# A preln attention and FFN block on one core: maxima split by two-input operations, the decay matrix in four loads behind a landed store of maxima, the end of the token stage inside the prime phase

## What is computed

```python
attn_scores = jnp.einsum('bhqd,bhkd->bhqk', q, k) / jnp.sqrt(jnp.float32(D))
time_diffs = jnp.abs(t[:, None] - t[None, :])
dp = jnp.clip(decay_params, 0.01, 0.9999)
decay_masks = dp[:, :, None, None] ** time_diffs[None, None, :, :]
decay_mask = jnp.einsum('hnqk,hn->hqk', decay_masks, softmax(mix_weights))
attn_scores = attn_scores * decay_mask[None]
attn_probs = jax.nn.softmax(attn_scores, axis=-1)
out = jnp.einsum('bhqk,bhkd->bhqd', attn_probs, v)
...
x = x + attn(layernorm(x))
x = x + ffn(layernorm(x))     # relu(x W1 + b1) W2 + b2, ternary W1 and W2
```

## Time and profile before

| | us |
|---|---|
| median of 3 runs | 1926.46 (1925.45 to 1927.16) |
| the profiled execution | 1931.35 |
| its span, first to last instruction | 1929.2 |
| TensorE busy | 1713.2, 89% |
| VectorE busy | 1533.6, 79% |
| ScalarE busy | 1435.0, 74% |
| GpSimd busy | 915.8, 47% |
| mean granted TensorE clock | 0.944 of full |

### The profile page before, as it was taken

The page is one execution under the profiler, slowest core; times in us unless marked ns, Lnnn a source line. Parts: engine busy times, 40 slices in busy tenths (PEclk is TensorE's granted clock), DMA queues, the critical chain, the costliest instruction groups (busy, mean ns, idle before and its releaser), DMA issues.

```text
span 1929.2 us, 31199 instructions
## 1 busy us (share of the span) xinstructions
PE 1713.2 (89%) x10834; PEld 587.6 (30%) x10834; DVE 1533.6 (79%) x2637; ACT 1435.0 (74%) x2670; POOL 915.8 (47%) x915
## 2 busy tenths in 40 slices
PE   7827999998989989989898989999899999898998
PEld 5401222222222222222232222222222222233666
DVE  5766888787878787878787878888787878797885
ACT  6534878687878787878787877788787878787655
POOL 6732637363646464554545463636363636443010
PEclk9957999899999999999899999999999999999999
DMA  6967574656656665758484847575747565572540
GB/s 209 324 215 171 151 166 132 163 138 162 155 141 153 152 159 138 181 125 192 113 200 121 184 129 163 151 169 138 173 121 173 144 164 146 135 198 58 157 124 33
DMA packets 181389, 299.99 MB, mean 155 GB/s; under 512 B 90576, under 2 KB 114000, under 8 KB 166992
## 3 DMA queue, kind: packets, MB, share of 16 engines
q1 hardware_dynamic: 175152, 296.81, 60.7%
q10 hardware_dynamic: 6080, 1.19, 0.4%
HBM read 152.18 MB, written 42.99 MB: 101 GB/s over the span
## 4 chain that ended last, share of the span: by engine, by line
PE 59%; DVE 15%; issue 9%; DMA 5%; SPq 3%; ACT 2%; POOL 1%; DVEq 0%; ACTq 0%
PE tile L1611 21%; PE ring L1626 20%; PE ring L1580 11%; DVE masked L1376 5%; DMA q_stack<-max_rows 4%; DVE unseen L1376 4%; DVE max_parts L1394 3%; SPq L149 2%; PE tile L1608 2%; PE ring L1696 2%; PE tile L1678 1%; ACT probs L1330 1%; DVE qk L1463 1%; DMA q_stack<-lo 1%; DMA table_in<-table_scratch 1%
## 5 line engine op out<-in xcount | busy, mean ns | idle before, releaser
L1330 ACT ACTIVATE probs<-tile 128x512 f32<-128x512 f32 x2048 | 1107.7, 603 | 339.8 <-PE tile L1611 228.1
L1376 DVE CUSTOM_DVE_ANT_0 masked<-ring,mask 128x1024 f32<-128x1024 f32 x512 | 625.4, 1222 | 180.1 <-PE ring L1580 160.6
L1611 PE MATMUL tile<-q_stack,k_stack 98*128 98x512 f16 (+2 forms) x2560 | 648.3, 340 | 75.4 <-issue 54.9
L1376 DVE CUSTOM_DVE_ANT_0 unseen<-ring,mask 128x1024 bf16<-128x1024 f32 x512 | 625.4, 1221 | 111.7 <-PE ring L1580 111.6
L1626 PE MATMUL ring<-probs,v_ones 128*32 128x512 f32 x4096 | 575.8, 635 | 0.1
L1158 POOL COPY diag<-masked 128x128 f32<-128x128 f32 x512 | 150.1, 293 | 795.3 <-DVE part_max L1376 785.1
L1580 PE MATMUL ring<-k_raw,q_raw 64*128 64x512 f16 x2048 | 353.8, 399 | 98.5 <-DVE part_max L1376 72.5
L1611 PEld LDWEIGHTS tile<-q_stack,k_stack 98*128 98x128 f16 x2560 | 201.6, 99 | 716.3 <-ACT probs L1330 454.8
L213 POOL TENSOR_TENSOR decayed<-qk,table_in 128x1024 f32<-128x1024 f32 x120 | 284.1, 2367 | 9.3 <-DMA table_in<-table_scratch 9.3
L232 POOL TENSOR_TENSOR lo<-decayed,hi 128x1024 f16<-128x1024 f32 x120 | 256.3, 2136 | 0.0
L1580 PEld LDWEIGHTS ring<-k_raw,q_raw 64*128 64x128 f16 x2048 | 91.6, 94 | 277.9 <-DVE part_max L1376 150.5
(11 more groups left out here) (151 smaller groups left out, 1001.9 us busy)
## 6 DMA issues: line engine op xcount, KB each, us to landing
mask<-mask_row_scratch SPq DMA_DIRECT2D x32, 1984.0 KB, 19.9
k_stack<-hi SPq DMA_DIRECT2D x128, 256.0 KB, 5.2
q_stack<-hi SPq DMA_DIRECT2D x256, 128.0 KB, 4.7
table_in<-table_scratch SPq DMA_DIRECT2D x64, 256.0 KB, 8.5
q_raw<-raw_scratch SPq DMA_DIRECT2D x128, 128.0 KB
k_stack<-lo SPq DMA_DIRECT2D x64, 256.0 KB, 4.2
q_stack<-lo SPq DMA_DIRECT2D x128, 128.0 KB, 3.9
out_scratch<-heads_out SPq DMA_DIRECT2D x64, 256.0 KB, 5.7
```

The lines of the kernel that those rows point to most:

```text
L1330: nc.scalar.activation(probs[:, (2 * s + x // 2) % 4, x % 2 * 512:(x % 2 + 1) * 512], tile[:, n % TILE_BANKS], ACT.Exp, scale=1.0 / (SCALE ...
L1376: nc.vector.tensor_tensor_reduce(out=masked[:, b % 2] if diagonal else unseen[:], in0=pair, in1=factor, scale=1.0, scalar=-3.0e38, op0=ALU ...
L1611: last = nc.tensor.matmul(out, k_stack[h][:, level, kb * P:(kb + 1) * P], q_stack[h][:, half, level, first - half * HALF:first - half * HA ...
```

## The change

Three parts.

1. `split_max`: `hi` is computed by an operation with a second input, a zero broadcast from a 128 x 1 tile, instead of by one with a single input.
2. The mask of a head is loaded by 4 DMAs of 128 x 992 elements instead of one of 128 x 3968. SP waits for a landed store of maxima in three places of a step: for that of slot 5 before `load_max_pass(0, i + 1)`, for that of slot 21 before `load_max_pass(1, i + 1)`, and for that of slot 29 before `builder.load(i + 2)`.
3. The tiles for q, k, v and raw rows live in a tensor that outlasts the token block (`Projections`; second stacks and `probs` lie over it later). GpSimd's splits and SP's raw stores of the last two groups, and the v, k and q stores of the last group, are issued at the start of the attention block. Only the first `k_stack` gets its constants from ScalarE; the second by a DMA from the first, for which SP waits until all rows and raw rows have landed. `builder.load(1)` moves ahead of the raw stores and of two level loads.

```diff
 def load_head_mask(sp, row, mask, head, done):
-    sp.dma_start(mask[:], bass.AP(row.tensor, head * 2 * SEQ + 1, [[1, P], [1, MASK]])).then_inc(done, QUADS)
+    width = MASK // MASK_DMAS
+    for c in range(MASK_DMAS):
+        sp.dma_start(mask[:, c * width:(c + 1) * width],
+                     bass.AP(row.tensor, head * 2 * SEQ + 1 + c * width, [[1, P], [1, width]])).then_inc(done, QUADS)
...
-            for g in range(GROUPS):
-                store_v(g)
+            for g in range(GROUPS - 1):
+                proj.store_v(sp, g)
...
-            store_raw(GROUPS - 1)
             sp.wait_ge(later_in, 2 * QUADS)
...
-            for g in range(GROUPS):
-                split_raw(g)
+            for g in range(GROUPS - proj.LAST):
+                proj.split_raw(pool, g)
...
+            proj.store_v(sp, GROUPS - 1)
+            proj.store_qk(sp, GROUPS - 1)
             for x in range(2):
                 builder.load_levels(sp, x)
-            builder.wait_stores(sp)
             load_max_pass(1, 0)
+            proj.wait_rows(sp, GROUPS // BATCH)
             load_v(0, 0)
+            builder.load(sp, 1)
+            for g in range(GROUPS - proj.LAST, GROUPS):
+                proj.store_raw(sp, g)
             for x in range(2):
                 load_q(0, 1, x)
-            builder.load(sp, 1)
+            sp.wait_ge(const_ready, 1)
+            proj.wait_rows(sp, GROUPS)
+            proj.wait_raw(sp, GROUPS)
+            sp.dma_start(k_stack[1][STACK:STACK + MAXROWS], k_stack[0][STACK:STACK + MAXROWS]).then_inc(const_in, QUADS)
...
                 if more:
+                    sp.wait_ge(rows_in, QUADS * (UNITS * i + 2))
                     sp.wait_ge(ring_free, items_done(BLOCKS - 1 - LEAD, o))
                     load_max_pass(0, i + 1)
...
                 if more:
+                    sp.wait_ge(rows_in, QUADS * UNITS * (i + 1))
                     sp.wait_ge(ring_free, items_done(SLOTS - 1 - LEAD, o))
                     load_max_pass(1, i + 1)
...
                 if i + 2 < STEPS:
+                    sp.wait_ge(rows_in, QUADS * (UNITS * (i + 1) + 1))
                     builder.load(sp, i + 2)
...
             pool.sem_inc(diag_ready, 1)
+            for g in range(GROUPS - proj.LAST, GROUPS):
+                proj.split_raw(pool, g)
             for s in range(-LEAD, 0):
                 keep_diag(s, 0)
...
-            builder.wait_stores(act)
-            for h in range(2):
-                rows = k_stack[h][STACK:STACK + MAXROWS].rearrange("p l x -> p (l x)")
-                nc.scalar.copy(rows, unit[STACK:STACK + MAXROWS].broadcast_to([MAXROWS, DEPTH * SEQ])
-                               ).then_inc(const_ready, 1)
+            rows = k_stack[0][STACK:STACK + MAXROWS].rearrange("p l x -> p (l x)")
+            nc.scalar.copy(rows, unit[STACK:STACK + MAXROWS].broadcast_to([MAXROWS, DEPTH * SEQ])).then_inc(const_ready, 1)
...
             store_max_rows(0, 0, TURN_SLOT - UNIT_SLOTS, 0)
+            proj.wait_rows(act, GROUPS)
...
-                nc.vector.tensor_scalar(hi, row, -1.0 / MAXUNIT, None, ALU.mult).then_inc(max_hi, 1)
+                nc.vector.scalar_tensor_tensor(out=hi, in0=row, scalar=-1.0 / MAXUNIT,
+                                               in1=zero[:].unsqueeze(2).broadcast_to([P, DEPTH, UNIT_SLOTS]),
+                                               op0=ALU.mult, op1=ALU.add).then_inc(max_hi, 1)
```

More of the change, by code:

```diff
@@ L47 @@
 RAW_DMAS = 8
+MASK_DMAS = 4
 ROWS = DECAYS * HEAD_DIM
@@ L233, in rest, with token_block @@
                                      self.half_view(self.hi[:, level], level, side), ALU.subtract).then_inc(self.lo_ready, 1)
-def token_block(nc, a, keep, builder, scr):
+def token_block(nc, a, keep, builder, proj, scr):
     ident, wo_hi, wo_lo = keep["ident"], keep["wo_hi"], keep["wo_lo"]
@@ L364, in load_first_raw @@
             def load_first_raw():
-                for u in range(2):
-                    sp.wait_ge(raw_stored[u], HALF_GROUPS // 2 * 2 * QUADS)
+                proj.wait_raw(sp, HALF_GROUPS)
                 load_raw_head(sp, scr["raw"], builder.q_raw, builder.k_raw, 0, 0, builder.raw_in)
@@ L811, in score_parts, with attention_and_ffn_block @@
     return [p for p in parts if p[1] // HALF == side]
-def attention_and_ffn_block(nc, a, keep, builder, scr, out):
+def attention_and_ffn_block(nc, a, keep, builder, proj, scr, out):
     ident, wo_hi, wo_lo = keep["ident"], keep["wo_hi"], keep["wo_lo"]
@@ L827, in sem @@
             return ctx.enter_context(nc.semaphore(name))
-        q_stack = [builder.q_stack, sb("q_stack1", [STACK + MAXROWS, 2, DEPTH, HALF], F16)]
-        k_stack = [builder.k_stack, sb("k_stack1", [STACK + MAXROWS, DEPTH, SEQ], F16)]
-        probs = sb("probs", [P, 4, HALF])
+        q_stack, k_stack = ([first, second] for first, second in zip((builder.q_stack, builder.k_stack), proj.stacks()))
+        probs = proj.probs()
         mask = [builder.mask, sb("mask1", [P, MASK])]
@@ L1812, in build @@
                                   lambda name: scores.enter_context(nc.semaphore(name)))
-            token_block(nc, a, keep, builder, scr)
-            attention_and_ffn_block(nc, a, keep, builder, scr, out)
+            proj = Projections(nc, scr, lambda name, shape, dt=F32: scores.enter_context(nc.sbuf_tensor(name, shape, dt)),
+                               lambda name: scores.enter_context(nc.semaphore(name)))
+            token_block(nc, a, keep, builder, proj, scr)
+            attention_and_ffn_block(nc, a, keep, builder, proj, scr, out)
 def kernel(**inputs):
```

139 lines of the change are left out of this document (84 added, 55 removed).

## The result

| | before | after |
|---|---|---|
| median us (range) | 1925.95 (1919.73 to 1927.16) | 2003.22 (1999.89 to 2006.08) |
| ratio | 1 | 1.0388, 95% interval 1.0359 to 1.0417 |
| profiled execution, its span | 1931.35, 1929.2 | 1999.89, 1998.1 |
| step 0 begins, step 1, step 15 | 159.65, 268.36, 1681.99 | 152.26, 267.60, 1743.14 |
| a step, mean of 1 to 14 | 101.0 | 105.4 |

The change makes the kernel 77 us slower. I had forecast slower, by 40.5. The time forecast was 1967, and 2003.2 lies 1.8 us under the upper end of the range, 2005.

What follows compares the result with a forecast made beforehand. Bound taken: TensorE's attention chain with VectorE's maxima, and TensorE's waits for stores of maxima. +49 for 14 steps and -8.5 for the prime phase, +40.5 on 1931.35, give 1971.9, as a median 1967; range 1865 to 2005.

Steps and rivals of the forecast that it cites:

- the slot-0 stall: Start of a step: level loads wait behind raw and mask loads on two engines, a new stall of some 5 us.
- Part 1, nothing either way: Maxima's first operation in two-input form: no gain or loss; bounds a loss under 1 us and a gain of 58 us.
- The slot-24 stall goes: TensorE's wait at slot 24 for the slot-21 store of maxima disappears: 4.5 us, plus 2.6 us of slow clock.
- From S to the next step, 34.8: From issue of the slot-21 store of maxima (S) to the next step's start: 34.8 us against 36.2; bounds 30 to 37.
- the 26.0: Time for a head's raw and mask loads on two engines, 26.0 us, taken unchanged from the trace before.
- The slot-29 wait: SyncE's wait before the next build's loads: delays them and head 1's 18 level loads behind them; no size of its own.
- Slots 8 and 16: Start times within a step: slot 8 at 26.2 us instead of 23.2, slot 16 at 52.2 instead of 48.4.
- rival (3): Small stores slip through at slots 8 and 16; a step within 1.5 us of 101, 1900 to 1935 us; chance 0.24.
- A step: Each step takes 104.5 us against 101.0, 3.5 slower; 14 steps give +49.
- Part 3, -8.5: Token-stage end moved: third maxima block 3.5 us earlier, step 0's table wait gone; gain 8.5 us, bounds 3 and 13.
- (2): Level loads at the step start don't wait; 106 us off, 1820, or 1850 if a part stays; chance 0.16.
- (4): The two-input maxima operation doesn't wait for GpSimd, nor does what follows; up to 58 us less; some 3 in 100.

Runs made afterwards that it cites:

- the direct comparison: Raw loads on 16 engines and moved token-stage end, without DMA waits or mask pieces: two-input first maxima operation 1795.3 us against 1793.9 with one input.
- before_wait21: Kernel before plus only the wait for the landed slot-21 store before the second load_max_pass: 2081.6 us, ratio 1.0814.
- no_wait29: Changed kernel without the wait for the slot-29 store before the next build's loads: 2053.8 us, ratio 1.0674 to the kernel before.
- no_part2: Changed kernel with one mask DMA and none of the three new waits: 1922.7 us, ratio 0.9995 to the kernel before.

## Why the prediction was right, and where its size was off

The direction was right and so was the mechanism of the slot-0 stall. The size was not: the range reached the result by 1.8 us, and it did so though the start of the next step and part 3 lay outside their own bounds and the tail was no term at all.

*Part 1, nothing either way.* Held: the chain's share for it is 2%, and the direct comparison shows no difference.

*The slot-24 stall goes.* Held. In after slots 23 and 24 last 2.75 and 3.16 us on average, against 6.66 and 4.47.

*From S to the next step, 34.8.* Right in mechanism, short in size. SP starts the raw loads 2.3 us after the slot-21 store (forecast 2.6). Raw and mask take 29.2 us, not the 26.0 that I carried over from rows of before. From their landing to the first exponential it is 6.1 (forecast 6.2). So 37.6 instead of 34.8, over the upper bound of 37, against 36.2 before: what I took for a gain of 1.4 was a loss of 1.4. The failed term is the 26.0, which measured 29.2: it was read off a stretch of which the last part left the two engines nearly alone, and was moved to one where the level loads and the heads' store keep all 16 busy and a packet takes 1.5 times as long. That the same stretch takes 34.5 in before_wait21 and 35.0 in no_wait29 shows that it depends on what moves beside it, not on the bytes.

*The slot-29 wait.* I had it as a delay of the build's loads and as nothing else. It is a delay (with raw on 16 engines it costs some 20 us), and in after it also keeps that traffic off the two engines, worth 50 us. The prediction had no such term.

*Slots 8 and 16.* Over-estimated. By the mean slot lengths slot 8 starts at 25.4 (forecast 26.2, before 23.2), slot 16 at 51.1 (52.2, before 48.5), and S is at 67.8 (69.7, before 64.8). Of the 2.2 us at slot 8, slot 0 with its slow clock has 1.55 (4.29 against 2.74) and slots 5 to 7 have 0.7. So slot 8 went by what rival (3) said, and not by the slot-5 store, for which TensorE has no wait there. Slot 16's wait did grow. A slip in the sum itself is small: 28.6 + 6.4 is 35.0, not the 35.3 from which the times behind it are counted.

*A step.* 105.4 against a forecast of 104.5: the two misses have opposite signs, 2.8 and 1.9, so it is partly luck that the step is only 0.9 off. Over 14 steps the forecast is short by 13 us.

*Part 3, -8.5.* Wrong, and outside its bounds of 3 and 13: step 1 begins 0.8 us earlier in after, and 1.3 (267.08) in no_part2, which has none of part 2. The prime phase did get its gain: VectorE's third block begins at 124.19 instead of 129.63 (forecast 126.1), and step 0 begins 7.4 us earlier, in the other profiles with this part and raw on two engines 2.4 to 6.0. I had followed the moved work up to the first score product and no further. But slot 5 of step 0 grew from 11.0 to 15.9 us. These are the rows of the chain of after there:

```profile
158.71 11.89 DMA raw_scratch<-late
...
170.68 0.64 SPq L1097
...
178.65 2.69 DMA late<-lo
```

I had named this ordering in the prediction ("SP waits until the last raw stores have landed, then for one more small DMA") and had charged it only a part of the 8.33 us for the table. ScalarE's cast, which waits 12.8 us there against 8.0 before, was not in the sum. Together this is +7.7 against the forecast; what the rest of it is I haven't traced.

*Step 15 and the tail.* +7.7, which I hadn't looked at. TensorE waits 3.71 us at 1766.05 in it, in slot 7, and before has no such wait in its last step. It stands before slot 8, which needs the store of slot 5; this goes out at 1760.00, so TensorE goes on 9.8 us behind it. Slot 0 takes 1.3 us more, with the slow clock of the stall ahead of it. The rest I didn't trace.

Together, 13 + 7.7 + 7.7 = 28 of the miss; the remaining 8 are the distance between the profiled executions and the medians.

*What was to show it.* The slot-24 wait gone and one at slot 0 in every step (15 times), a level load that lands in 12.9 us instead of 3, waits at slot 16, a low clock in the first slots (slot 0 takes 4.29 us instead of 2.74): all seen. In steps 1 to 14 there is no wait for a DMA at slot 8, which I had named too.

*The rivals.* (2) is out: the level loads do wait. (3), that small stores slip through, is right at slot 8 and wrong at slot 16, where the stall was to go and grew from 11 to 22.2 us; its time, 1900 to 1935, is out. (4) is out by the direct comparison.

## What to carry to other kernels

A duration read from a quiet stretch of a DMA queue isn't valid in a busy one: before moving a transfer, look at the DMA share around it and at what moves there, before and after the move. If a few low-share transfers set the order of everything behind them, first look at how many engines they use; here one dimension of an access pattern was worth 6.8%, while waits placed around it moved it by 1.3 to 8.1% the wrong way. And follow each moved item up to every engine that consumes its buffer: most of the gain ahead of step 0 was lost at a cast on ScalarE, five slots later.

## What was not expected of the hardware

- With raw loads on two engines and the share of all 16 over 0.9, a packet of 4096 bytes takes 0.25 us instead of 0.176, one of 15872 bytes 0.92 instead of 0.60, and the windows shown have 206 to 281 GB/s. With the mask alone on all 16 engines its rows take 0.61 us at share 1.02, and the rate is 423 GB/s.
- The 16 KB store of maxima, 66 packets, is through so fast with an empty queue that SyncE issues the next load 2.3 us behind it; among the packets of raw and mask loads it takes 8.65 to 11.7 us.
- Holding back later loads by one wait (the slot-29 wait; two of 512 KB and four of 256 KB, and what follows them) shortened earlier transfers on the same queue from 35.0 to 29.2 us: being first in the queue doesn't protect a transfer that uses few engines.
